# Muon loops of a test-time-training layer in another order, their sums as passes of halves, and a first stage that reads in quarters

## What is computed

```python
qkv = x @ qkv_w + qkv_b                       # q, k, v: 2048 x 128 each; q and k are normalized by head, scaled, shifted
theta = {gate: 128 x 512, val: 128 x 512, proj: 512 x 128}
def loss_fn(p):
    h = swish(k @ p['gate']) * (k @ p['val'])
    return mean((h @ p['proj'] - v) ** 2)
for _ in range(2):
    grads = jax.grad(loss_fn)(theta)
    theta = {n: theta[n] - 0.1 * newton_schulz(grads[n]) for n in theta}   # 5 iterations
h_q = swish(q @ theta['gate']) * (q @ theta['val'])
o = h_q @ theta['proj'] @ proj_w + proj_b
```

## Time and profile before

| | us |
|---|---|
| median of 3 runs | 1672.77 |
| range of them | 1665.45 to 1678.71 |
| the profiled execution, device time | 1683.69 |
| its span, first to last instruction | 1681.4 |
| first loop of Ttt, from its first product to the border's sums | 1151.2 to 1264.7 |
| second loop | 1293.9 to 1402.3 |
| first scan of Mamba starts | 84.8 |

### The profile page before, as it was taken

How to read it: one execution, slowest core, us unless ns; L and a number is a source line. 1 busy time by engine, 2 the same in 40 slices (tenths; PEclk the granted TensorE clock), 3 DMA queues, 4 the chain that set the end, 5 groups by cost and what they waited for, 6 DMA issues and landing times.

```text
span 1681.4 us, 24800 instructions
## 1 busy us (share of the span) xinstructions
PE 1254.4 (75%) x9098; PEld 792.9 (47%) x9098; DVE 1045.1 (62%) x1915; ACT 676.6 (40%) x1275; POOL 656.7 (39%) x657
## 2 busy tenths in 40 slices
PE   5457777513777368878878559997998999965997
PEld 2123333311444134444446524454666666854996
DVE  7899999871211498878743454546665665642775
ACT  2744343210334137767741235554334234321442
POOL 1277878567366360000003330024641441043453
PEclk9679889856888579999968789998999999986998
DMA  6247567111232441211001141115000000001113
GB/s 221 103 161 258 212 233 267 55 43 49 70 81 67 151 145 39 64 57 44 16 15 31 44 154 54 38 35 220 1 1 1 1 1 1 1 31 40 37 47 95
DMA packets 75448, 133.84 MB, mean 80 GB/s; under 512 B 12723, under 2 KB 39670, under 8 KB 74688
## 3 DMA queue, kind: packets, MB, share of 16 engines
q1 hardware_dynamic: 66400, 115.97, 20.8%
q0 software_dynamic: 8064, 13.87, 2.6%
q10 hardware_dynamic: 864, 2.43, 0.4%
HBM read 96.22 MB, written 38.38 MB: 80 GB/s over the span
## 4 chain that ended last, share of the span: by engine, by line
PE 47%; issue 19%; DVE 13%; POOL 8%; ACT 5%; SPq 3%; DMA 3%; another core or an unknown queue 2%; POOLq 0%; DVEq 0%; ACTq 0%
PE ps L1840 6%; POOL sb_arena L1044 5%; PE ps L3956 3%; DVE sb_arena L1906 3%; PE ps L2207 2%; ACT sb_arena L2154 2%; PE ps L2190 2%; PE ps L2449 2%; PE ps L3115 2%; SPq L68 1%; PE ps L3131 1%; PE ps L658 1%; PE ps L3923 1%; PE ps L3924 1%
## 5 line engine op out<-in xcount | busy, mean ns | idle before, releaser
L1906 DVE TENSOR_REDUCE sb_arena<-ps 128x2 f32<-128x1024 f32 (+2 forms) x192 | 211.0, 1130 | 58.2 <-PE ps L2435 33.7
L2154 ACT ACTIVATE sb_arena<-ps 128x512 f32<-128x512 f32 (+1 forms) x320 | 160.3, 554 | 57.9 <-PE ps L2207 54.4
L658 PE MATMUL ps<-sb_arena,sb_const 128*128 128x512 f32 x256 | 136.1, 677 | 27.9 <-DVE sb_arena L852 27.9
L846 DVE TENSOR_TENSOR_SCAN sb_arena<-ps,sb_arena 128x1024 f32<-128x1024 f32 x64 | 145.0, 2279 | 4.0 <-ACT ps L945 3.1
L1938 POOL CAST sb_arena<-sb_arena 128x8 bf16<-128x8 f32 (+2 forms) x32 | 6.5, 203 | 289.4 <-DVE sb_arena L1906 148.8
L1840 PE MATMUL ps<-sb_arena 128*32 128x256 f32 (+3 forms) x1856 | 117.2, 361 | 0.2 <-ACT sb_arena L2388 0.2
L1566 POOL DMA_INDIRECT y<-sb_arena x80 | 77.7, 972 | 61.1 <-ACT sb_arena L1515 41.1
L658 PEld LDWEIGHTS ps<-sb_arena,sb_const 128*128 128x128 f32 x256 | 55.9, 220 | 93.1 <-issue 53.5
L1143 POOL DMA_INDIRECT xe<-sb_arena x80 | 78.5, 981 | 51.8 <-issue 29.2
L1044 POOL TENSOR_TENSOR sb_arena<-sb_Wreg,sb_arena 128x1024 f32<-128x1024 f32 x32 | 78.0, 2458 | 40.4 <-DMA sb_arena<-bcrows 32.2
L3776 POOL TENSOR_TENSOR sb_arena<-sb_arena 128x512 f32<-128x512 f32 x32 | 40.7, 1271 | 124.5 <-DVE sb_arena L3380 124.5
(11 more groups left out here) (519 smaller groups left out, 3233.7 us busy)
## 6 DMA issues: line engine op xcount, KB each, us to landing
sb_arena<-bcrows SPq DMA_DIRECT2D x80, 512.0 KB, 6.4
xe<-sb_one SPq DMA_DIRECT2D x31, 260.0 KB, 8.9
sb_Wreg<-e0w SPq DMA_DIRECT2D x24, 256.0 KB, 7.1
sb_arena<-xe SPq DMA_DIRECT2D x16, 325.0 KB
y<-sb_zero SPq DMA_DIRECT2D x20, 256.0 KB, 6.9
sb_arena<-y SPq DMA_DIRECT2D x4, 1024.0 KB, 9.3
sb_Wreg<-e1w SPq DMA_DIRECT2D x16, 256.0 KB, 2.7
sb_Wreg<-e3gu SPq DMA_DIRECT2D x1, 4096.0 KB, 12.5
```

What stands on the lines that cost most here:

```text
L658: t = e.matmul(k.b(self.Y + c), k.c("ident"), self.hc[i % 4][:, c * 512:(c + 1) * 512], start=False, stop=n == 15)
L846: e.tensor_tensor_scan(self.hh[i % 3], k.pair(2 * (i % 2)).rearrange("p c t -> p (c t)"), self.dB[i % 3], 0.0, MUL, ADD).then_inc(S.scan.s ...
L1906: e.tensor_reduce(dst, src, AX.X, MAX).then_inc(S.mxr.sem, 1)
L2154: e.activation(self.PT[s % 4][:, 2 * h:2 * h + 2, 0:n], bank[:, :, 0:n], ACT.Exp, scale=self.scale).then_inc(S.ex.sem, 1)
```

## The change

**Start and Mamba.** x comes in four transfers of 4 tiles, and statistics, roots, reciprocals and normalized tiles go by groups of 4 in a new order. ACT loads the table of square roots before it waits for statistics. POOL's items 1 and 2 of the scan wait until all four pieces of du are there.

**Ttt.** c is written as sg * val part + s1 * h. DVE makes the first term itself (`slope_dve`, signal q), POOL the product s1 * h and the sum (`slope_pool`). The value product of tile i+1 now waits for q. The sums over tiles 0 to 14 are three passes of halves each: ACT rounds dv and dg (`high_act`), POOL subtracts to get dv's low part (`low_pool`), DVE dg's (`low_dve`); keys are split once for every four tiles (`key_act`, `key_pool`). The last tile's sums stay fp32. The orders of all queues change, keys' and queries' side work is spread wider, and the copies of keys and gradients lie in the memory of the last stage's weights, so that these are loaded only after the last fp32 sum (`acc` 32).

```diff
@@ Start.sp
-        for b in range(2):
-            e.dma_start(k.X[:, 8 * b:8 * b + 8, :], xin[:, 8 * b:8 * b + 8, :]).then_inc(k.g_x[b].sem, 16)
+        for c in range(4):
+            e.dma_start(k.X[:, 4 * c:4 * c + 4, :], xin[:, 4 * c:4 * c + 4, :]).then_inc(k.g_x[c].sem, 16)
@@ Mamba.dve
-        w.wait_ge(k.g_x[0], 16)
-        tile_stats(k, e, w, range(0, 8), S.stats)
+        self.stats_dve(e, w, 0)
+        self.stats_dve(e, w, 1)
         self.norm_dve(e, w, 0)
-        w.wait_ge(k.g_x[1], 16)
-        tile_stats(k, e, w, range(8, 16), S.stats)
+        self.norm_dve(e, w, 1)
+        self.stats_dve(e, w, 2)
         self.feature_dve(e, w, 0)
+        self.stats_dve(e, w, 3)
         self.feature_dve(e, w, 1)
-        self.norm_dve(e, w, 1)
-        w.wait_ge(S.rs, 2)
+        self.norm_dve(e, w, 2)
+        self.norm_dve(e, w, 3)
+        w.wait_ge(S.rs, 4)
@@ Mamba.act
+        load_table(k, e, 7, ACT.Sqrt, self.eps[:, 0:1])
@@ Mamba.pool
-            w.wait_ge(S.du, 2 * b + eb + 1)
+            w.wait_ge(S.du, 4 if i in (1, 2) else 2 * b + eb + 1)
@@ Ttt.sp
+        fill_rows(k, e, w, k.xe7, k.filled)
+        w.wait_ge(self.S.acc, 32)
         load_w(k, e, "e3")
-        fill_rows(k, e, w, k.xe7, k.filled)
@@ Ttt: sums on PE
+    def sum_pe(self, e, bank, i, high, low):
+        kh, kl = self.keyH[:, i, :], self.keyL[:, i, :]
+        e.matmul(bank, kh, high, start=i == 0, stop=False)
+        e.matmul(bank, kl, high, start=False, stop=False)
+        return e.matmul(bank, kh, low, start=False, stop=False)
@@ Ttt.pe, one iteration
                 if i < NT:
-                    self.fwd_pe(e, w, g0 + i, i)
+                    self.gate_pe(e, w, g0 + i, i)
+                if 1 <= i <= NT:
+                    self.pred_pe(e, w, g0 + i - 1)
+                if i < NT:
+                    self.value_pe(e, w, g0 + i, i)
                 if 1 <= i <= NT:
-                    self.pred_pe(e, w, g0 + i - 1)
-                if i >= 2:
-                    self.acc_pe(e, w, g0 + i - 2, i - 2)
-                if 1 <= i <= NT:
-                    self.back_pe(e, w, g0 + i - 1, i - 1)
+                    self.sum_proj_pe(e, w, g0 + i - 1, i - 1)
+                    self.back_pe(e, w, g0 + i - 1)
+                if step == 0 and i in self.PAIRS:
+                    self.keys_pe(e, w, self.PAIRS.index(i))
                 if i < NT:
                     self.trans_pe(e, w, g0 + i)
+                if 2 <= i <= NT:
+                    self.sum_value_pe(e, w, g0 + i - 2, i - 2)
+                    self.sum_gate_pe(e, w, g0 + i - 2, i - 2)
@@ Ttt.dve, one iteration (all new order)
+                if i >= 2:
+                    self.low_dve(e, w, g0 + i - 2)
+                if i:
+                    self.pred_dve(e, w, g0 + i - 1, i - 1)
                 if i < NT:
+                    self.a_dve(e, w, g0 + i)
+                if i:
                     self.rest_dve(e, w, g0 + i - 1)
+                if i < NT:
+                    self.h_dve(e, w, g0 + i)
+                    self.slope_dve(e, w, g0 + i)
+                if step == 0 and i in self.PAIRS:
+                    self.keys_rest_dve(e, w, 1 + self.PAIRS.index(i))
+                if i:
+                    self.value_dve(e, w, g0 + i - 1)
+                    self.gate_dve(e, w, g0 + i - 1)
@@ Ttt: new on DVE, ACT and POOL
+    def slope_dve(self, e, w, g):
+        e.tensor_tensor(self.c_[x], self.sg[x], k.b(4), MUL).then_inc(S.q.sem, 1)
+    def low_dve(self, e, w, g):
+        w.wait_ge(S.eH, self.sums(g))
+        w.wait_ge(S.acc, g - 1)
+        e.tensor_tensor(self.dgL[x], self.dg[x], self.dgH[x].bitcast(F32), SUB).then_inc(S.eL.sem, 1)
+    def high_act(self, e, w, g):
+        w.wait_ge(S.acc, g - 1)
+        w.wait_ge(S.dv, g + 1)
+        e.copy(self.dvH[x], self.dv[x]).then_inc(S.vH.sem, 1)
+        w.wait_ge(S.dg, g + 1)
+        e.copy(self.dgH[x], self.dg[x]).then_inc(S.eH.sem, 1)
+    def slope_pool(self, e, w, g):
+        w.wait_ge(S.s1, g + 1)
+        w.wait_ge(S.h, g + 1)
+        w.mark(e.tensor_tensor(self.s1[x], self.s1[x], self.h_[x], MUL))
+        w.own()
+        w.wait_ge(S.q, g + 1)
+        e.tensor_tensor(self.c_[x], self.c_[x], self.s1[x], ADD).then_inc(S.c.sem, 1)
+    def low_pool(self, e, w, g):
+        w.wait_ge(S.vH, self.sums(g))
+        w.wait_ge(S.acc, g - 1)
+        e.tensor_tensor(self.dvL[x], self.dv[x], self.dvH[x].bitcast(F32), SUB).then_inc(S.vL.sem, 1)
```

More of the change, by code:

```diff
@@ L721, in pe, with stats_dve, norm_dve @@
         self.project_out(e, w, 1)
-    def norm_dve(self, e, w, b):
+    def stats_dve(self, e, w, c):
+        w.wait_ge(self.k.g_x[c], 16)
+        tile_stats(self.k, e, w, range(4 * c, 4 * c + 4), self.S.stats)
+    def norm_dve(self, e, w, c):
         k, S = self.k, self.S
-        h = slice(8 * b, 8 * b + 8)
-        w.wait_ge(S.sd, b + 1)
+        h = slice(4 * c, 4 * c + 4)
+        w.wait_ge(S.sd, c + 1)
         e.reciprocal(self.rs[:, :, h], self.sd[:, :, h]).then_inc(S.rs.sem, 1)
[L729 to L732, removed]
+        w.wait_ge(S.rs, c + 1)
+        for i in range(4 * c, 4 * c + 3):
+            e.tensor_scalar(self.xn[:, i, :], k.X[:, i, :], k.lnmv[:, i, 0:1], self.rs[:, 1, i:i + 1], SUB, MUL).then_inc(S.xnv.sem, 1)
     def feature_dve(self, e, w, c):
@@ L949, in act @@
         w.wait_ge(S.eps, 1)
-        for b in range(2):
-            h = slice(8 * b, 8 * b + 8)
-            w.wait_ge(S.stats, b + 1)
+        load_table(k, e, 7, ACT.Sqrt, self.eps[:, 0:1])
+        for c in range(4):
+            h = slice(4 * c, 4 * c + 4)
+            w.wait_ge(S.stats, c + 1)
             e.activation(self.sd[:, 0, h], k.lnmv[:, h, 1], ACT.Sqrt, bias=self.eps[:, 0:1])
@@ L1032, in pool @@
         e.memset(self.eps[:, 1:2], 1e-10).then_inc(S.eps.sem, 1)
[L1033 to L1036, removed]
+        for c in range(4):
+            i = 4 * c + 3
+            w.wait_ge(S.rs, c + 1)
+            e.tensor_scalar(self.xn[:, i, :], k.X[:, i, :], k.lnmv[:, i, 0:1], self.rs[:, 1, i:i + 1], SUB, MUL).then_inc(S.xnp.sem, 1)
         self.stack_pool(e, w)
@@ L1458, in deviations_act @@
         w.wait_ge(k.g_const, 16)
[L1459 removed]
+        w.wait_ge(self.before.S.stats, 5 + b)
         e.activation(self.sd[:, h], k.lnmv[:, h, 1], ACT.Sqrt, bias=k.c("eps")).then_inc(S.sd.sem, 1)
@@ L3019, in __init__ @@
         self.dpH, self.dpL = ([parts[:, 3072 + 256 * y + 128 * x:3200 + 256 * y + 128 * x] for x in range(2)] for y in range(2))
+        parts = k.halves("a3sums", -12288, 8192)
+        self.keyH, self.keyL = (parts[:, 2048 * x:2048 * (x + 1)].rearrange("p (i d) -> p i d", d=128) for x in range(2))
+        self.dvH, self.dvL, self.dgH, self.dgL = ([parts[:, 4096 + 1024 * y + 512 * x:4608 + 1024 * y + 512 * x] for x in range(2)] for y in range(4))
         self.hq = [x.rearrange("p (b t) -> p b t", b=4) for x in (spare[:, 0:2048], spare[:, 2048:4096])]
@@ L3693, in act @@
             g0 = 16 * step
-            for i in range(NT + 2):
+            for i in range(NT + 1):
                 if i < NT:
-                    self.fwd_act(e, w, g0 + i)
+                    self.sigmoid_act(e, w, g0 + i)
+                    self.rest_act(e, w, g0 + i)
+                if i == NT:
+                    load_table(k, e, step, ACT.Sqrt)
+                if i:
+                    self.back_act(e, w, g0 + i - 1)
                 if step and i == 0:
@@ new lines, in beside_pool, with query_pool @@
+        if i in (1, 5, 9):
+            self.keys_pool(e, w, 1 + i // 4)
+        if i in (2, 6, 10):
+            self.values_pool(e, w, 1 + i // 4)
+        if i in (3, 7, 11, 13):
+            c = (3, 7, 11, 13).index(i)
+            q = self.qkv[:, 4 * c:4 * c + 4, 0:128]
+            w.wait_ge(S.qv, 2 * c + 2)
+            e.tensor_tensor(q, q, k.s("qkv_b")[:, 0:128].unsqueeze(1).to_broadcast([128, 4, 128]), ADD).then_inc(S.qb.sem, 1)
+    def query_pool(self, e, w, i):
+        k, S, c = self.k, self.S, i // 4
+        xh = self.heads(0, c)
+        if i % 4 == 1:
+            w.wait_ge(S.qm, c + 1)
+            w.mark(e.tensor_tensor(xh, xh, self.wide("qn_s"), MUL))
+        if i % 4 == 2:
+            w.own()
+            e.tensor_tensor(xh, xh, self.wide("qn_b"), ADD).then_inc(S.qn.sem, 1)
+        if i % 4 == 3:
+            xs = k.X[:, 4 * c:4 * c + 4, :]
+            e.tensor_tensor(xs, xs, self.pb.unsqueeze(1).to_broadcast([128, 4, 128]), ADD).then_inc(S.xb.sem, 1)
```

171 lines of the change are left out of this document (88 added, 83 removed).

## The result

The changed kernel takes **1651.66 us** (median of 6 runs, 1646.35 to 1661.88); the kernel before took 1672.28 beside it (6 runs, 1663.37 to 1680.99). The ratio is 0.9875, 95% interval 0.9841 to 0.9909: faster by 1.25%. The profiled executions are 1661.88 (span 1660.07) and 1683.69: 21.8 us apart. I had forecast 1659, 13.9 less; the range held the time, and the forecast gain was too small by a third.

The account below looks back on a forecast made before the run. PE, busiest in both Ttt loops, was taken as the main bound. Start -2.5, POOL's items -4.0, second loop -4.4 and first loop -3.0 sum to -13.9 us, giving 1659 us on the median of 1672.77; range 1643 to 1681.

Parts of the forecast that it names:

- Start: First stage up to the projection: x in quarters and the early table start the projection 2.5 us earlier, range 1.0 to 3.0.
- the start's gain is not there: Rival, first stage: quarters land no earlier and scans 1 and 2 wait for POOL; 6.5 shrinks to 2.5, 1663; chance 0.13.
- POOL's items 1 and 2: Before the first scan: holding POOL back returns two stretched DVE products to 1.23 each; 4.0 us less, bounds 1.5 and 4.5.
- PE's sums: Both Ttt loops: passes of halves at 0.23 replace fp32 products, taking PE's tile from 6.09 to 5.75 us.
- Second loop: Second Ttt loop: shorter tiles -3.0, waits for c gone -1.8 and -3.2, query products +3.6; sum -4.4 us.
- The query products at +0.9 each: Second loop: DVE's four products for the queries lie on its critical cycle with part of a lock; +3.6 in all.
- First loop: First Ttt loop: shorter tiles -3.0, first wait for c -1.4, split-key waits -4.0, DVE side work +5.4; sum -3.0 us.
- The +5.4 for side work on the ring: First loop: DVE's side work of 10.9 us less 5.5 of slack lengthens the loop by 5.4.
- The ring: Ttt loops: DVE's order makes a cycle from dp through dg, ACT's rounding and the low part; 5.26 us a tile plus B.
- B: Ttt loops: time per tile that DVE's low part of dg waits for POOL; 0 to 1.0 us, small without side work.
- PE sets the pace everywhere: Rival, Ttt loops: 5.75 us a tile, second loop -9.4, first -8.8, total -24.7, so 1648; chance 0.22.
- The ports' lock makes the ring the bound: Rival, Ttt loops: the low part waits for POOL every tile; period 6.6, 1695, or 1680 at half; chance 0.20.

Follow-up runs that it names:

- a1: The kernel before with the new start alone, without POOL's wait for du and with the old Muon loops; first scan 2.7 us earlier, no measurable time gain.
- a4: The kernel before with the Muon loops' new order and sums in passes of halves, old first stage; 14.4 us less (interval 5.7 to 18.7).
- b1: The changed kernel with its new order, but both sums as fp32 products again, without roundings, low parts and split keys; 1599.09 us, ratio 0.9849.
- c2: The changed kernel with DVE's low part of dg moved behind the slope's product, in front of dv; Muon loops under 1 us shorter than the kernel before.
- b3: The changed kernel with DVE's low part of dg moved behind h, in front of the slope; ratio 0.9813 against the kernel before.

## Why the prediction was right, and where it was short

**Start.** Forecast -2.5, measured -1.85 at the projection. The step that failed is the quarters' landing: 1.2 earlier held for the first alone, the second came at 7.23. That this gain "carries" is shown up to the first scan (2.7 in a1); behind it 0.4 or 0.9 us are left, too few to be told from the spread of the marks. In a1's trace, 1.5 us go in one gap, behind scan 8 (8.37 against 6.88 in a4), but with both edits that gap is anything from 6.17 to 7.94. The rival "the start's gain is not there" did not come: the first quarter lands earlier, scans 1 and 2 wait for nothing, and start and wait together gave 7.3 at the first scan and 7.1 by the means at scan 31, against its 2.5 and my 6.5.

**POOL's items 1 and 2.** Forecast -4.0, measured -4.1: from DVE's first sum (L785 before) to the first scan are 32.0 to 32.1 us in the kernel before, a1 and a4, and 27.9 to 28.1 with the wait. "Next to nothing is given back" held: at scan 31 the gain is 5.7.

**PE's sums.** PE's work in a tile was forecast at 5.75, and the tile taken at 5.9; 5.80 was found, and 5.55 and 5.95 with a pass less and with one fp32 product. The price of 0.23 a pass was right, and PE does pace the plain tiles. That this saves 16 x 0.19 in each loop was the wrong conclusion. Against the same order with fp32 sums it saves nothing in the second loop and costs 5.1 in the first. The sum came out near the truth partly by luck, since two mistakes stood against each other: too little gain for the order, too little loss for the late tiles. What was left of them is most of what the forecast lacks: by the later runs the loops gave 13.1, not 7.4.

**Second loop, -4.4 forecast, -7.2 measured.** Row by row: from the first product to the first dp 10.06 before and 6.87 after, -3.2 where I had -1.8. I counted the wait for c, but not that the value product itself (three passes) no longer stands in front of the first prediction. The 15 tiles from dp to dp fell from 94.2 to 90.4, -3.8, where my terms give -2.6 (-3.0, -3.2, +3.6). The missing 1.2 is the plain tile, 5.80 where I took 5.9. The query products at +0.9 each were sized about right: 1.0 to 1.2.

**First loop, -3.0 forecast, -4.8 measured.** Again the beginning: 10.48 to 7.97, -2.5 against -1.4. The tiles gave -2.2 against -1.6. The +5.4 for side work on the ring was too small: the 15 intervals from dp to dp are 96.7, 9.7 more than 15 tiles of 5.80. In b1, with the same side work and no low part, they are 91.3, not more than 15 of its 6.12. It was hidden by the other mistake, since the order alone gives 10.8 and I had credited it with 5.4.

**The ring and B.** I had B at 0 to 1.0 and small in plain tiles: by the subtraction's length over 0.68 it is 0.2 there, 0.5 on average, up to 1.09 in late ones. That 1.20 is just the mean at which I said the forecast would be wrong. What I did not see is that the ring has 0.4 to spare (dp waits that long for PE) in plain tiles and nothing where one more instruction stands in front of the low part. The page SBUF — State Buffer of the Trainium skill, section Who interferes with whom, on which I leaned, says that the second to issue is blocked; the trace agrees (1.47 behind POOL, 0.69 ahead of it), and a place 0.6 us earlier in the order turns it round.

**The rivals.** "PE sets the pace everywhere" had the loops at -8.8 and -9.4 and 1648 in all; the time lies between it and the forecast. Its plain tile is the one found; its late tiles, +2 and +1, are not. "The ports' lock makes the ring the bound" did not come in the changed kernel, but c2 shows such a lock: 6.61 a tile, where I had worked out 6.6. There the low part stands in another place and PE waits for it in front of the sum, so that the equal number is luck.

## What to carry to other kernels

Split a change of order and of arithmetic before crediting either: here the order gave all of the loops' gain, and the cheaper products only paid once one DVE instruction had moved. Where DVE and POOL both read SBUF, look for a place in which DVE's instruction starts first, and keep anything that waits for another engine from standing in front of the instruction on which PE hangs. A gain before a long stage that several engines share has to be read behind that stage, and there over several profiles: here places behind 31 scans differ by 2.6 us for the same code.

## What the runs showed of the hardware

A DVE instruction with a single SBUF operand is held up by POOL as well. L3402 adds a constant to 128x64, and took 0.19 in the earlier trace rows (as L3366); in the changed kernel, timeline of DVE and then POOL:

```profile
1172.78 1.15 DVE L3402 TENSOR_SCALAR sb_arena<-sb_arena 128x64 f32<-128x64 f32 x1
1173.97 0.55 DVE L3404 RECIPROCAL sb_arena<-sb_arena 128x64 f32<-128x64 f32 x1
1174.56 1.11 DVE L3406 TENSOR_TENSOR sb_arena<-sb_arena 128x512 f32<-128x512 f32 x1
```
```profile
1172.59 1.29 POOL L3853 TENSOR_TENSOR sb_arena<-sb_arena 128x512 f32<-128x512 f32 x1
1173.84 1.27 POOL L3859 TENSOR_TENSOR sb_a3sums<-sb_arena,sb_a3sums 128x512 fp32r<-128x512 f32 x1
```

It starts 0.19 after POOL and ends with it. The reciprocal beside it ran in 0.55 while POOL was inside its next instruction. In b3 the same addition took 0.86, begun 0.48 after POOL. In all traces this addition of 128x64 took 0.18 to 0.20 where POOL was idle or within 0.03 of its end, and 0.86 to 1.16 where POOL was inside a product.

And DVE's wait of 5.70 or 1.11 us before scan 52 hung on which of its two levels the clock was at in one stretch of 4 us (0.50 or 1.00), the same code having met either.
